# Scores ahead of the turned probabilities in each slot of the matrix engine, and group 2's key transfers on one queue

## The reference, cut to what matters

```python
# first attention ("magnitude")
sr = (einsum('bhqd,bhkd->bhqk', qr, kr) + einsum('bhqd,bhkd->bhqk', qi, ki)) * scale
si = (einsum('bhqd,bhkd->bhqk', qi, kr) - einsum('bhqd,bhkd->bhqk', qr, ki)) * scale
probs = softmax(sqrt(sr * sr + si * si), axis=-1)
ctx = einsum('bhqk,bhkd->bhqd', probs, v)
# second attention ("causal")
scores = where(causal, einsum('bhqd,bhkd->bhqk', q, k) / sqrt(D), NEG_INF)
y = einsum('bhqk,bhkd->bhqd', softmax(scores), v)
# then top-2 of 8 experts, capacity 1280 tokens each
```

## Time and profile before

| | before |
|---|---|
| median of 3 runs | 1014.57 (1010.95 to 1019.37) |
| profiled execution | 1020.76 |
| its span, first to last instruction | 1019.0 |
| busy in the span: PE / PEld | 900.7 (88%) / 701.8 (69%) |
| busy: DVE / ACT / POOL | 654.1 (64%) / 647.2 (64%) / 508.7 (50%) |
| mean granted clock of TensorE | 0.916 of full |

### The profile page before, as it was taken

One profiled execution on the slowest core, in us unless ns is written; L12 is line 12 of the kernel. 1 busy time (PEld: TensorE's weight loads), 2 busy tenths in 40 slices (PEclk: granted clock), 3 DMA queues, 4 the chain that ended last, 5 costly groups with the idle time before them and its releaser, 6 DMA issues.

```text
span 1019.0 us, 21583 instructions
## 1 busy us (share of the span) xinstructions
PE 900.7 (88%) x7037; PEld 701.8 (69%) x7038; DVE 654.1 (64%) x3059; ACT 647.2 (64%) x1379; POOL 508.7 (50%) x557
## 2 busy tenths in 40 slices
PE   3377969899999979999999999467999999999996
PEld 3254546566666656677776776256999999999896
DVE  1676788998998877688877767673344344343341
ACT  2046768886989988888988889264345345344441
POOL 7677756766221201143334333405677677677654
PEclk7567888998999978999999999757999999999999
DMA  7344323232110200010111102436455456555442
GB/s 202 59 73 78 48 47 49 62 64 32 32 33 3 62 1 2 2 38 2 38 38 38 36 5 69 74 55 108 62 110 99 78 109 89 88 108 91 53 52 32
DMA packets 63300, 59.12 MB, mean 58 GB/s; under 512 B 17471, under 2 KB 54242, under 8 KB 63202
## 3 DMA queue, kind: packets, MB, share of 16 engines
q0 software_dynamic: 26880, 29.46, 20.0%
q1 hardware_dynamic: 36130, 28.18, 10.8%
q10 hardware_dynamic: 192, 0.26, 0.1%
HBM read 35.18 MB, written 16.39 MB: 51 GB/s over the span
## 4 chain that ended last, share of the span: by engine, by line
PE 63%; DVE 13%; ACT 5%; issue 3%; POOL 1%; DMA 1%; POOLq 0%; DVEq 0%; ACTq 0%
PE ps_scores L796 14%; PE ps_ring L788 11%; PE ps_ring L1066 10%; PE ps_ring L796 6%; PE ps_ctx L925 5%; PE ps_scores L908 5%; PE ps_scores L1066 4%; PE ps_scores L911 3%; DVE probs L1454 2%; DVE probs L1468 1%; ACT probs L1168 1%; DVE k L1375 1%; PE ps_ring L871 1%; PE ps_ctx L788 1%; ACT high_hot L1261 1%
## 5 line engine op out<-in xcount | busy, mean ns | idle before, releaser
L1290 ACT ACTIVATE probs<-ps_scores,fc_bias 128x512 f32<-128x512 f32 (+1 forms) x144 | 88.9, 617 | 171.8 <-PE ps_scores L796 156.6
L659 POOL DMA_INDIRECT out<-z_t,slots_now x80 | 128.0, 1600 | 82.9 <-DVE z_t L1807 58.8
L1150 ACT ACTIVATE prob_t<-ps_ring 128x512 f32<-128x512 f32 x192 | 114.5, 597 | 35.7 <-PE ps_ring L788 34.7
L788 PE MATMUL ps_ring<-ident,probs 128*128 128x128 f32 x768 | 127.8, 292 | 7.9 <-DVE x_hi L1346 3.6
L1159 ACT ACTIVATE square<-ps_scores 128x512 f32<-128x512 f32 x192 | 105.0, 601 | 32.5 <-PE ps_scores L908 27.4
L1175 ACT ACTIVATE probs<-probs,neg_max 128x128 f32<-128x128 f32 x384 | 120.7, 397 | 2.6 <-DVE neg_max L1454 2.5
L1454 DVE CUSTOM_DVE_ANT_0 probs<-ps_scores,causal 128x128 f32<-128x128 f32 x384 | 88.5, 286 | 40.8 <-PE ps_scores L911 40.3
L1066 PE MATMUL ps_ring<-work,probs 128*128 128x192 f32 x672 | 114.5, 326 | 0.0
L788 PEld LDWEIGHTS ps_ring<-ident,probs 128*128 128x128 f32 x768 | 91.3, 148 | 33.0 <-issue 15.6
L1066 PEld LDWEIGHTS ps_ring<-work,probs 128*128 128x128 f32 x672 | 109.3, 190 | 0.1
L1448 DVE CUSTOM_DVE_ANT_0 probs<-square 128x128 f32<-128x128 f32 x384 | 89.4, 287 | 29.7 <-ACT square L1159 26.9
(11 more groups left out here) (232 smaller groups left out, 2082.5 us busy)
## 6 DMA issues: line engine op xcount, KB each, us to landing
work<-pj_w SPq DMA_DIRECT2D x8, 576.0 KB
k<-k_signed SPq DMA_DIRECT2D x128, 32.0 KB
token_in<-xin SPq DMA_DIRECT2D x8, 384.0 KB, 3.4
out<-resid SPq DMA_DIRECT2D x8, 384.0 KB, 4.2
vals<-fc_w SPq DMA_DIRECT2D x8, 384.0 KB
vals<-fc_w SPq DMA_DIRECT2D x16, 192.0 KB
k<-k_signed POOLq DMA_DIRECT2D x48, 32.0 KB, 2.0
out<-z_t,slots_now POOLq DMA_INDIRECT x80, 3.6
```

Source lines behind the costliest of these rows:

```text
L659: gp.indirect_dma_start(out[:, :], bass.IndirectOffsetOnAxis(slots_now[:, u, 1, t:t + 1], 0), slot_y[:, o, :], None, compute_op=ALU.add).t ...
L788: return pe.transpose(dst, src, ident[0:n, 0:n])
L1150: sc.activation(prob_t[:, s % 2, :, :], src.rearrange("p (h q) -> p h q", h=4), ACT.Exp if p is mag else ACT.Copy).then_inc(ring_free[i], 1)
L1290: sc.activation(hidden[:, c % 2, f_, 0:128 * nt], ps_scores[:, i, 0:128 * nt], ACT.Gelu, bias=fc_bias[:, e, f_:f_ + 1]).then_inc(gelu_done ...
```

## The change

Two things change.

First, on PE alone, a slot now has the order S, T, V, F: the block that issues `scores` is moved ahead of the one that issues the first fill. In slots without S nothing moves. ACT, DVE and POOL keep their order of jobs. The semaphores and what is waited for stay as they are.

Second, a constant `ALONE = 2` says up to which group SP issues all key transfers. Groups 1 and 2 now have 24 on SP; before, only group 1 had. POOL issues none for group 2. The waits count accordingly.

```diff
+ALONE = 2
...
         def wait_for_turned_keys(eng, b, g):
-            eng.wait_ge(keys_turned[b], 16 * (8 * g if b == 0 else 4 + 4 * g))
-            if b > 0 and g > 1:
-                eng.wait_ge(late_turned[b - 1], 16 * 4 * (g - 1))
+            late = max(0, g - ALONE) if b > 0 else 0
+            eng.wait_ge(keys_turned[b], 16 * (8 * g - 4 * late))
+            if late:
+                eng.wait_ge(late_turned[b - 1], 16 * 4 * late)
...
-                    for quarter, part in product(range(4 if b == 0 or g == 1 else 2), range(2)):
+                    for quarter, part in product(range(4 if b == 0 or g <= ALONE else 2), range(2)):
...
-                if 2 <= p + 1 < GROUPS:
+                if ALONE < p + 1 < GROUPS:
                     turn_rest_of_keys(p + 1)
...
                 for slot in range(STEPS):
                     fills = fills_of(p, slot)
-                    if ready is not None and slot < JOBS:
-
-                        fill(*fills.pop(0))
                     if now is not None and 0 <= slot - SCORE_SLOT[phase_of(now)[0].name] < JOBS:
                         scores(now, slot - SCORE_SLOT[phase_of(now)[0].name])
+                    if ready is not None and slot < JOBS:
+
+                        fill(*fills.pop(0))
```

More of the change, by code:

```diff
@@ L933, in one_pass @@
                     fills = fills_of(p, slot)
+                    if now is not None and 0 <= slot - SCORE_SLOT[phase_of(now)[0].name] < JOBS:
+                        scores(now, slot - SCORE_SLOT[phase_of(now)[0].name])
                     if ready is not None and slot < JOBS:
                         fill(*fills.pop(0))
-                    if now is not None and 0 <= slot - SCORE_SLOT[phase_of(now)[0].name] < JOBS:
-                        scores(now, slot - SCORE_SLOT[phase_of(now)[0].name])
                     turned = ready is not None and ready < GROUPS and slot == 1
```

## The result

The changed kernel takes 1120.11 us (median of 4 runs, 1115.28 to 1126.12) against 1016.9 for the kernel before (4 runs, 1010.95 to 1019.37) in the same comparison. The ratio is 1.1002, with a 95% interval from 1.0955 to 1.1048: slower by 10%, 103 us. The forecast was 1088 with a range from 1055 to 1128.

The account below looks back on a forecast made before the run. It took the ACT and PE exchange to bound the magnitude passes and PE the causal ones. Magnitude +63 and causal +10 gave +73 us, on the 1014.57 median 1088 us, range 1055 to 1128.

Parts of the forecast that it names:

- What bounds the kernel: Magnitude passes: ACT and DVE nearly full, squares and scores pace a 1.92 us slot; causal passes: PE busy 237 of 249 us.
- The ring: Magnitude passes, job 0 to 10: scores, T, ACT's copy and squares wait in turn, 3.16 us a step against 1.92.
- the copy to the first square: Link of the ring on ACT, from the copy of T to the first square, put at 0.70 us.
- +63 at full clock in the magnitude passes: Sum of the ring's losses over passes 1 to 7, with the key stall's end counted in pass 2.
- The clock stays up: Likeliest case: PE keeps full clock with small losses in the lengthened magnitude slots, 1062 to 1110 us; chance 0.62.
- rival 1: Clock falls in the lengthened magnitude slots, about 4.0 us a step, 1115 to 1143 us; chance 0.22.
- steps near 4: Sign in the magnitude passes that the forecast is wrong because of the clock: steps near 4 us, not about 3.15.
- Pass by pass: Ten magnitude steps: 31.6 us in most passes, 33.9 in pass 4, 31.6 to 32 in pass 7, about 32.5 in pass 1.
- Keys: Group 2 key transfers: the 5.5 us stall in pass 2 goes, and comes back by a microsecond at worst.
- Causal passes: No ring there, only longer seams on PE behind each F: +10 us, with 0 and +13 as ends.
- The seam sum: Causal slots behind an F: PE's sequence takes 1.40 us instead of 1.20, up to 0.2 a slot.
- Rivals 2, 3 and 4: 2: slack returns in slots 12 to 1, 1051 to 1060, 0.13; 3: DVE regains waits, 1010 to 1025; 4: nothing; together 0.03.

Follow-up runs that it names:

- act_swapped: The changed kernel with ACT taking the two squares ahead of the copy of T in the magnitude slots: 1020.89 us, ratio 1.006 to the kernel before.
- warm: The changed kernel plus four unread identity transposes in each of slots 2 to 10 of passes 1 to 7: 1075.57 us, ratio 1.0597 to before.
- lead_causal: The kernel before with scores ahead of T in the causal slots only, key transfers as before: 1025.35 us, ratio 1.0124.
- split_warm: The changed kernel with T between the two score pairs in magnitude slots, plus three unread transposes per slot 2 to 10, passes 1 to 7: 1143.21 us.

## Why the prediction was right or wrong

- **What bounds the kernel**: right. The magnitude passes hang on the exchange between ACT and PE, the causal ones on PE. Both showed in the runs that moved one engine's order at a time.
- **The ring**: right in its links and its place (act_swapped: 97 of 103 us gone), a little too large in size. The sum gave 3.16 a step, measured are 2.95. The term that was mis-sized is the copy to the first square, taken as 0.70 from the earlier trace rows. There the scores had started only 0.11 us ahead of the copy (270.04 and 270.15), so the squares could not follow it at once; here the scores are long done, and it is 0.49 (345.28 to 345.77). The other terms fit: T's first weight load to the copy 0.69 (344.59 to 345.28), the squares 1.08.
- **+63 at full clock in the magnitude passes**: warm, at full clock nearly throughout, is 61 above before by its ratio; less the causal 11.6 and with the keys' 3 back, about 52 are left for the ring, and by the traces the seven stretches are 55 longer than before. The smaller step accounts for the difference to within a few us: 0.21 in some 65 steps is 14. Two of the lengths it started from were also short: pass 1 was put at 25.1 today and pass 3 at 19.3, and from job 0 to job 10 they last 26.5 and 19.8.
- **The clock stays up**: this is the step that failed. It was given 0.62 and rival 1 got 0.22; what happened is rival 1 near its lower bound, with a little over half of the steps at the lower clock (for half of them 1115 was worked out). The prediction's own sign, steps near 4, showed in five of seven passes. warm prices it: 41 to 45 us, for which the sum had nothing. A step at the lower clock was put at about 4.0 and is 3.93. The rows could not decide between the two, but seven lengthened passes were seven chances to lose the clock, and a forecast at the upper level for all seven asked for more than open evidence gave. With the step's smaller size the magnitude passes come to 52 and another 41 to 45 in place of 63. That 1120 still lies in the range is in part luck: the range had taken in the lower half of rival 1, and the ring's sum was 11 too high, which made up for a quarter of what the clock cost.
- **Pass by pass**: ten steps took 29.8 and 29.9 in passes 5 and 7, where 31.6 and up to 32 were forecast; the others went to 35 to 44, with the clock at 0.54 to 0.66.
- **Keys**: the stall went in the changed kernel, as said, and SP's 24 issues took 15.42 us against 15.5 worked out. In slots of the old length it leaves 2.4 us for job 2, which the estimate had excluded only because the slots would be longer. It is worth 3 us alone and nothing measurable in the changed kernel.
- **Causal passes**: +10 forecast, +11.6 measured with an interval of 10 to 15 us. The seam sum was right; the waits of PEld show it as seams ahead of the values (+11.4) and of the scores (+3.5), less those ahead of transposes (-2.6), together +12.3, with the scores' waits for DVE nearly unchanged (8.4 and 9.5).
- **Rivals 2, 3 and 4**: no time came back in slots 12 to 1, DVE's wait for scores was not lost time (lead_causal), and T did come into the ring.

## What to carry to other kernels

When work is reordered on one engine, look at the queue of the engine that consumes it: an instruction that moves ahead on PE gains nothing if ACT's list still wants the other one first, and then a hidden transfer becomes a link of the ring. Write the ring down link by link from single rows; take a link's duration from a row where its start was not held up by something else. And when a change thins out PE's work, price the lower clock in the likeliest case as well, not only as a rival: here it was nearly as large as the ring itself (41 to 45 us against some 52).

## What the runs showed of the hardware

- 252 added transposes of 128x128 made the changed kernel 41 to 45 us faster; the granted clock was 0.89 to 1.00 in the ten steps of passes that had 0.54 to 0.66 without them.
- The busy share of PE does not tell whether the clock is granted. split_warm ran pass 3 at 0.50 with PE busy for 30.00 of 30 us, and pass 6 at 1.00 with steps of the same make-up; the changed kernel kept 0.94 in pass 5 with no weight load on PE for 1.1 us in a step of 2.95.
- In the rows shown at the upper clock, a change of PE between products on 32-row tiles, on full tiles and on 32-column tiles leaves 0.13 to 0.33 us without a weight load. Moving one block of four across another added about 1.5 us of such seams a causal pass.
